# A GNN kernel's edge sort: four fifths moved from one-hot matmuls to indirect transfers into a DRAM table

## The reference, cut to what matters

```python
# GIN, twice:  agg[d] = sum over edges (s -> d) of h[s]
agg = jax.ops.segment_sum(h[src], dst, num_segments=n_nodes)
z = jax.nn.relu((agg + h) @ Wa + ba) @ Wb + bb
# attention, per edge, softmax over the edges of one head:
e = leaky_relu(sum((concat(x[head], x[tail]) @ W) * relation_emb[edge_type]))
alpha = softmax of e over each head;  agg[head] += alpha * x[tail]
```

## Time and profile before

| | |
|---|---|
| median of 3 runs | 5086.33 us (5085.47 to 5087.33) |
| profiled execution, span from first to last instruction | 4502.2 us |
| instructions | 61902 |
| mean granted TensorE clock | 0.671 of full speed |

### The profile page before, as it was taken

The page is one execution under the profiler, slowest core; times in us unless marked ns, Lnnn a source line. Parts: engine busy times, 40 slices in busy tenths (PEclk is TensorE's granted clock), DMA queues, the critical chain, the costliest instruction groups (busy, mean ns, idle before and its releaser), DMA issues. The chain is left out here.

```text
span 4502.2 us, 61902 instructions
## 1 busy us (share of the span) xinstructions
PE 3040.5 (68%) x16266; PEld 2267.0 (50%) x16267; DVE 3392.0 (75%) x7111; ACT 2104.7 (47%) x5569; POOL 1731.0 (38%) x1694
## 2 busy tenths in 40 slices
PE   5888888887255555555435555555546888779878
PEld 2444444466255555555435555555535888435434
DVE  8888888842588888888668888888858885444345
ACT  4555555551344444444345555555527885132231
POOL 0000000062577777777277777777700000021010
PEclk7999999988555555555555555555555555889988
DMA  0000000030322222222122222222230000000000
GB/s 21 0 0 0 0 0 0 0 161 1 69 67 67 67 67 67 67 67 69 31 71 66 69 67 67 67 67 67 63 162 1 1 1 2 11 4 1 4 9 8
DMA packets 136540, 183.42 MB, mean 41 GB/s; under 512 B 48763, under 2 KB 110116, under 8 KB 135396
## 3 DMA queue, kind: packets, MB, share of 16 engines
q0 software_dynamic: 50048, 77.77, 7.6%
q1 hardware_dynamic: 85348, 84.60, 6.9%
q10 hardware_dynamic: 896, 18.10, 0.9%
HBM read 158.02 MB, written 22.33 MB: 40 GB/s over the span
## 5 line engine op out<-in xcount | busy, mean ns | idle before, releaser
L1121 POOL DMA_INDIRECT adjacency<-dram_table,sorted_dst x1564 | 1555.9, 995 | 672.7 <-issue 425.8
L1148 PE MATMUL banks<-adjacency 128*128 x3520 | 779.5, 419 | 463.6 <-ACT adjacency L1180 463.6
L1148 PEld LDWEIGHTS banks<-adjacency 128*128 128x128 f32 x3520 | 759.3, 332 | 507.2 <-issue 507.2
L1193 ACT ACTIVATE adjacency<-adjacency 128x128 f32<-128x128 bf16 x1760 | 537.9, 397 | 50.2 <-DVE adjacency L1241 50.0
L1286 DVE TENSOR_REDUCE adjacency<-adjacency 128x512 f32<-128x2048 f32 x110 | 399.5, 3632 | 125.7 <-ACT adjacency L1193 125.7
L1180 ACT ACTIVATE adjacency<-adjacency 128x2048 f32<-128x2048 f32 x110 | 210.3, 1912 | 565.2 <-DVE adjacency L1218 565.2
L1921 PE MATMUL banks<-adjacency,cheb_parts 128*128 128x512 f16 (+1 forms) x2100 | 437.0, 367 | 52.5 <-ACTq L97 31.7
L665 ACT ACTIVATE adjacency<-banks 128x400 f32 x590 | 296.9, 503 | 318.6 <-PE banks L637 313.5
L1173 PE MATMUL banks<-ident,adjacency 128*128 128x128 f32 x440 | 122.6, 434 | 447.5 <-DVE adjacency L1286 447.5
L2190 POOL TENSOR_TENSOR cheb_y<-cheb_y,cheb_gain 128x512 f32<-128x512 f32 (+1 forms) x21 | 24.1, 1150 | 984.2 <-DVE cheb_y L2106 984.2
L634 PE MATMUL banks<-cell_hot,src_hot 128*128 128x400 f16 x1180 | 319.7, 353 | 74.0 <-DVE cell_hot L572 73.0
(11 more groups left out here) (497 smaller groups left out, 6100.8 us busy)
## 6 DMA issues: line engine op xcount, KB each, us to landing
adjacency<-dram_src_rows SPq DMA_DIRECT2D x440, 128.0 KB
adjacency<-dram_table,sorted_dst POOLq DMA_INDIRECT x1564, 2.5
dram_adjacency<-adjacency ACTq DMA_DIRECT2D x1, 17600.0 KB, 46.3
adjacency<-dram_adjacency SPq DMA_DIRECT2D x1, 15387.5 KB, 39.4
dram_table<-adjacency SPq DMA_DIRECT2D x8, 291.0 KB, 6.1
adjacency<-dram_adjacency SPq DMA_DIRECT2D x1, 2212.5 KB, 14.5
dram_nodes<-x_nodes SPq DMA_DIRECT2D x1, 800.0 KB, 4.3
x_nodes<-dram_nodes SPq DMA_DIRECT2D x1, 800.0 KB, 5.8
```

The lines of the kernel that those rows point to most:

```text
L1121: pool.indirect_dma_start(ring[:, j % (RG * TG), :], None, dram["table"], bass.IndirectOffsetOnAxis(ap=S.dst_i[:, j:j + 1], axis=0)).then_ ...
L1148: ins = pe.matmul(sums[b % 2][:, s * W1:(s + 1) * W1], reach[:, b % 3, s, t, :], ring[:, bass.ds(at_r[s], TG), :][:, t, 0:W1], start=(t == ...
L1193: ins = act.activation(reach[:, b % 3, s, t, :], hot[:, b % 2, s, :, t], ACT.Identity, scale=-FAR, bias=score[:, b % 2, s * TG + t:s * TG ...
```

## The change

**The sort** is split. `PG` = 157 groups (`PT` = 628 columns of edges) go another way; 39 groups (`LEFT_T` = 156 columns) stay with the one-hots. For the 628 columns GpSimd makes a payload of two fp16 numbers for each edge, VectorE makes the address in a DRAM table, `place_of` (lane times 782 plus tile), and GpSimd issues 628 indirect transfers of 128 elements of 4 bytes each into `dram_spread`, which SyncE has cleared with two transfers. At the group's start GpSimd waits for the group three earlier. At the end it waits for all and loads the table back into SBUF (`S.spread`). `sorted_edges` adds the loaded values to the one-hot part's.

**The loop** of `build_adjacency` now has turns of 15 steps with one group in each: 39 turns and a rest of 5 steps. Its registers are loaded for 5 steps at a time (`AT_ONCE`), so each turn has three `load_row` on VectorE, three on TensorE and nine on ScalarE. The pair buffers of the sort are single now, and the group's pieces stand at steps 0, 3, 6, 8, 9, 11 and 13 of the turn.

**The block bases** are made by VectorE inside the first convolution: four instructions at block 0 and one `scalar_tensor_tensor` of 782 columns at each block from 2 to 24, issued right behind `z` of that block.

GpSimd no longer takes part in the two meetings around `build_adjacency`.

```diff
+TURN, AT_ONCE = 15, 5
+ROUNDS = ASTEPS // TURN
+PG = NG - ROUNDS
+PT = PG * TG
+LEFT_T = TP - PT
 # rank_edges, on_sp
+        sp.wait_ge(k.V.sem, zeros_made[0])
+        for half in range(2):
+            sp.dma_start(clear[:, half * NT:(half + 1) * NT], zero[:, 0:NT // 2].bitcast(F16)).then_inc(zeros_out.sem, 16)
...
-    def lanes_dve(dve, half):
-    def tiles_dve(dve, half):
-    def rows_dve(dve, half):
+    def places_of(dve, half):
+        V = k.V
+        n = min(HALF, PT - half * HALF)
+        V(dve.tensor_copy(pos_i[:, 0, :], pos[:, half * HALF:(half + 1) * HALF]))
         V(dve.tensor_scalar(pos_i[:, 1, :], pos_i[:, 0, :], P - 1, None, ALU.bitwise_and))
         V(dve.tensor_scalar(pos_i[:, 0, :], pos_i[:, 0, :], 7, int(MARK) // P - 1, ALU.logical_shift_right, ALU.bitwise_and))
+        places_made.append(V.mark(dve.scalar_tensor_tensor(S.place_of[:, half * HALF:half * HALF + n], pos_i[:, 1, 0:n], float(NT),
+                                                           pos_i[:, 0, 0:n], ALU.mult, ALU.add)))
+    def rows_dve(dve):      # the same keys as before, for the last 156 columns alone, once
...
 # rank_edges, on_act, ahead of the second clearing
+        act.wait_ge(k.G.sem, payload_made[0])
+        act.wait_ge(zeros_out.sem, zeros_out.at(1))
 # rank_edges, on_pool
+        pool.wait_ge(cols_copied.sem, cols_copied.at(2 * RB - 1))
+        k.G(pool.tensor_scalar(S.payload[:, :, 0], dst_f[:, 0:PT], -float(NPAD // 2), None, ALU.add))
+        pool.wait_ge(k.V.sem, typed[0])
+        k.G(pool.tensor_scalar(S.payload[:, :, 1], src_b[:, 0:PT], -LO, None, ALU.add))
...
+        pool.wait_ge(k.V.sem, places_made[0])
+        for t in range(PT):
+            if t == HALF:
+                pool.wait_ge(k.V.sem, places_made[1])
+            g = t // TG
+            if t % TG == 0 and g >= LATE:
+                pool.wait_ge(scattered[(g - LATE) % TURNS].sem, scattered[(g - LATE) % TURNS].at(((g - LATE) // TURNS + 1) * TG - 1))
+            pool.indirect_dma_start(dram["spread"], bass.IndirectOffsetOnAxis(ap=S.place_of[:, t:t + 1], axis=0),
+                                    S.payload[:, t, :], None).then_inc(scattered[g % TURNS].sem, 16)
...
+        pool.dma_start(S.spread[:, :, :], dram["spread"].rearrange("(q c) v -> q c v", q=P)).then_inc(back.sem, 16)
 # build_adjacency
     def act_turn(act, turn, n):
-        first = turn * TURN
-        at_j = load_row(k, act, table[0:1, 1, bass.ds(first, n)], 0, NWIN - 1)
-        next_g = load_row(k, act, table[0:1, 0, bass.ds(first + AHEAD_R, n)], 0, TP - TGA)
-        next_j = load_row(k, act, table[0:1, 1, bass.ds(first + AHEAD_R, n)], 0, NWIN - 1)
+        for h in range(0, n, AT_ONCE):
+            now = turn * TURN + h
+            at_j = load_row(k, act, table[0:1, 1, bass.ds(now, AT_ONCE)], 0, NWIN - 1)
+            next_g = load_row(k, act, table[0:1, 0, bass.ds(now + AHEAD_R, AT_ONCE)], 0, TP - TGA)
+            next_j = load_row(k, act, table[0:1, 1, bass.ds(now + AHEAD_R, AT_ONCE)], 0, NWIN - 1)
+            for i in range(h, h + AT_ONCE):
...
 # block bases
-    for a in range(1, NB):
-        G(pool.tensor_scalar(beyond[:, :], place[:, :], S.block_start[:, a:a + 1], None, ALU.is_ge))
-        ins = pool.tensor_tensor(S.base[:, :], S.base[:, :], beyond[:, :], ALU.add)
+    def block(dve, a):
+        k.V(dve.scalar_tensor_tensor(S.base[:, :], place[:, :], S.block_start[:, a:a + 1], S.base[:, :], ALU.is_ge, ALU.add))
 # gin_conv, on_dve, stage 0
                 dve.tensor_tensor(z[:, i % R, :], psum[i % 2][:, 0:w], low[:, i % R, :], ALU.add).then_inc(z_made.sem, 1)
+                beside_dve(i)
 # sorted_edges
-    dve.tensor_copy(values[:, :, :], S.sorted[:, :, :])
-    dve.wait_ge(bases.sem, bases.at())
+    dve.wait_ge(back.sem, back.at())
+    dve.tensor_tensor(values[:, :, :], S.sorted[:, :, :], S.spread[:, :, :].rearrange("p t v -> p v t"), ALU.add)
```

More of the change, by code:

```diff
@@ L209, in rank_edges @@
     starts_made, starts_spread, cols_made = k.sig("starts_made"), k.sig("starts_spread"), k.sig("columns_made")
+    zeros_out, scattered, back = k.sig("spread_cleared", 16), [k.sig(f"tails{r}", 16) for r in range(TURNS)], k.sig("spread_in", 16)
+    zeros_made, typed, places_made, payload_made = [], [], [], []
     nodes_padded, nodes_in = k.sig("nodes_padded"), k.sig("nodes_in", 16)
@@ L360, in on_dve @@
                 dve.wait_ge(taken.sem, taken.at(i))
[L361 to L365, removed]
+                places_of(dve, 0)
             elif half == 1 and a == 14:
@@ L608, in pe_rows, with pe_tiles @@
+    def pe_rows(pe):
+        pe.wait_ge(group_valued.sem, 1)
         for t in range(TG):
-            ins = pe.matmul(part_v[0:ROWS, :], row_hot[:, 1 - g % 2, :, t], lane_value[:, 1 - g % 2, :, :, t], start=(t == 0), stop=(t == TG - 1))
+            ins = pe.matmul(part_v[0:ROWS, :], row_hot[:, :, t], lane_value[:, :, :, t], start=(t == 0), stop=(t == TG - 1))
         ins.then_inc(part_made.sem, 1)
-    def pe_tiles(pe, g, v, read, last=False):
-        b = 1 - g % 2
-        lanes = part[0:ROWS, b, v * P:(v + 1) * P]
+    def pe_tiles(pe, v):
+        lanes = part[0:ROWS, v * P:(v + 1) * P]
@@ L623, in pe_tiles @@
-        ins = pe.matmul(high_v[:, v * 256:(v + 1) * 256], lanes, tile_hot[0:ROWS, b, 512:768], start=False, stop=last and v == 1)
+        pe.matmul(low_v[v][:, :], lanes, tile_hot[0:ROWS, 0:512], start=False, stop=False)
+        ins = pe.matmul(high_v[:, v * 256:(v + 1) * 256], lanes, tile_hot[0:ROWS, 512:768], start=False, stop=False)
         if v == 1:
-            ins.then_inc(read.sem, 1)
+            ins.then_inc(tiles_read.sem, 1)
     def pe_turn(pe, turn, n):
-        first = turn * TURN
@@ L629, in pe_turn @@
-        at_j = load_row(k, pe, table[0:1, 1, bass.ds(first, n)], 0, NWIN - 1)
-        for i in range(n):
-            r = i % RING
-            pe.wait_ge(hot_made.sem, i + 1)
-            for t in range(TGA):
-                ins = pe.matmul(psum[r][:, 0:NB * WIN], one_b[:, r, :, t], one_c[:, r, t, :], start=(t == 0), stop=False)
-            ins.then_inc(hot_read.sem, 1)
-            pe.wait_ge(copied.sem, i + 1)
-            pe.matmul(psum[r][:, 0:NB * WIN], cst.ident16[:, :], A4[:, :, bass.ds(at_j[i], 1), :], start=False, stop=True).then_inc(done.sem, 1)
-            if n >= EACH:
-                g = i // EACH
-                if i % EACH == 0:
-                    pe_rows(pe, g)
-                else:
-                    pe_tiles(pe, g, i % EACH - 1, part_read)
+        for h in range(0, n, AT_ONCE):
+            at_j = load_row(k, pe, table[0:1, 1, bass.ds(turn * TURN + h, AT_ONCE)], 0, NWIN - 1)
+            for i in range(h, h + AT_ONCE):
+                r = i % RING
+                pe.wait_ge(hot_made.sem, i + 1)
+                for t in range(TGA):
+                    ins = pe.matmul(psum[r][:, 0:NB * WIN], one_b[:, r, :, t], one_c[:, r, t, :], start=(t == 0), stop=False)
+                ins.then_inc(hot_read.sem, 1)
+                pe.wait_ge(copied.sem, i + 1)
+                pe.matmul(psum[r][:, 0:NB * WIN], cst.ident16[:, :], A4[:, :, bass.ds(at_j[i - h], 1), :], start=False, stop=True).then_inc(done.sem, 1)
+                if n == TURN and i == ROWS_AT:
+                    pe_rows(pe)
+                elif n == TURN and i in SPREAD_AT:
+                    pe_tiles(pe, SPREAD_AT.index(i))
```

234 lines of the change are left out of this document (119 added, 115 removed).

## The result

The changed kernel took 6020.4 us in the median (6018.8 to 6020.7), the kernel before 5085.9 beside it: a ratio of 1.184 (1.182 to 1.185), 934 us slower. The prediction was 5192. The times come in two conditions.

What follows compares the result with a forecast made beforehand. Bound: the loop's chain of ScalarE copy, identity matmul and next copy. Loop +97, first convolution +13.5, small ones -5.1 give +105.4 on 5086.3: 5192 us, 8-in-10 range 5094 to 5265.

Steps and rivals of the forecast that it cites:

- I cost them at nothing: GpSimd's 628 transfers and their small writes, beside other work until the table is wanted at 1218 us: +0, at most +294.
- The runs' median lies 584.1 us above the span; I take that part as unchanged: Whole kernel: timed runs exceed the profiled span of 4502.2 us by 584.1, carried unchanged into the forecast time.
- That is 0.028 for a value, and 0.578 for 5: ScalarE's register loads in the loop: price per value, making three boundaries of a 15-step turn 7.73 us.
- The clock: Adjacency loop: mostly at half clock, a fifth of the time at 2.4 GHz, plain steps 1.28 us, mean near 0.6.
- Rival 1: Adjacency loop: the clock stays at 2.4 GHz, +11.4 us in all, a time of 5098; chance 0.13.
- VectorE off the path: Adjacency loop: VectorE does not set the pace; its pure step is some 0.67 us of the 1.28.
- The groups': Adjacency loop: 39 groups left of 196 on the one-hots, 157 x 0.31 = 49 us saved.
- The first convolution: VectorE's new instruction lengthens 23 blocks from 2.34 to 2.92 us: +13.5 us, bounds 0 and 23.
- The small ones: Rank stage, memsets, last group's tail and `sorted_edges`: small savings and costs summing to -5.1 us, bounds -8 and +3.
- the key operations: Rank stage, part of the small ones: fewer or narrower key operations on VectorE, said to save 4.1 us together.
- Rival 2: Attention layer waits for the table because GpSimd's transfers come late; at 2.3 us each +294, 5486 us; chance 0.10.
- Rival 3: Adjacency loop: register loads in the middle of a turn are hidden, loop -106 us, 4989 in all; chance 0.05.

Runs made afterwards that it cites:

- before_by_four: The kernel before with its register loads cut into fours, nothing else: 4482.3 against 4505.0 us (0.995) in the first condition, 5045.8 against 5067.3 (0.9955) in the second.
- twelve_by_four: The changed kernel with turns of 12 steps, loads of 4 values, 49 groups on TensorE: 4402.4 us against the kernel before's 4503.9; second condition 5675.6 against 5069.9.
- after_again: The changed kernel, unaltered, run again beside the kernel before, in the first condition: 4739.1 us against 4503.9, a ratio of 1.052.
- the execution of 5023.2 us: One of the four executions of `after_again`, the changed kernel unaltered; the other three took 4735.6 to 4741.6 us.
- before_again: The kernel before, unaltered, profiled once more: 4504.3 us with a span of 4502.7.

## Why the prediction was wrong, point by point

**"I cost them at nothing."** This is the step that failed in the measured times. Its own sum was right: 1.26 to 1.4 us for each, the last at about 920 us, wanted only at the end of the convolutions. What it left out is what the transfers do to the engines beside them: they hold up TensorE's hand-overs. I asked whether GpSimd would be late, and the place of the Trainium skill that I weighed ("SBUF — State Buffer", "Who interferes with whom") speaks of GpSimd kept waiting by VectorE. With the scatters beside the loop GpSimd was done by 923 us at the latest. The same section, which is about SBUF's ports, says that TensorE and ScalarE never wait on anyone; the hand-over of 6.5 us from one to the other beside the scatters is not in it. Price: 1755.4 - 1060.0 = 695 us of the 702; another 9 lie ahead of the first copy, which starts at 103.8 for 94.8 with the first scatters beside it.

**"The runs' median lies 584.1 us above the span; I take that part as unchanged."** Wrong as a reading. A span so far below its own kernel's times was the one sign in the profile that it was taken in another condition than the timed runs, and that something in the kernel was sensitive to it. From the first gather to the end the changed kernel loses 580 us by the condition and `before_by_four` 568, so the term nearly cancelled; had I asked what costs 584 us, the gathers were the candidate, and the change puts 628 of their kind beside the loop.

**"That is 0.028 for a value, and 0.578 for 5."** The line was drawn through loads of 2 and 12. What the runs show is 0.309 for 4 and 0.78 for 12 from a multiple of 4, 0.534 for 5 from such a place, 1.12 for 5 from another, 0.49 for 2. An estimate that fits all: from a first place that is a multiple of 4 the values come by fours, at some 0.24 to 0.31, and what is left singly at 0.22 to 0.25; from any other first place all come singly. The Trainium skill ("DMA: Bandwidth & Descriptors", "Latency and other measured facts") gives such a load a floor of about 600 ns; the trace doesn't agree (309 ns). The boundaries of four turns add up to 43.9 us, 10.97 a turn where I had 7.73: 39 x 3.24 = 126 us, and the loop was 1060.0 where I had 933. In the first condition this is the whole miss: 233 against 105.

**The clock** was right: plain steps at 1.28 us, those with spreading matmuls at 1.67, the one with the group at 1.89 for 1.85, a mean of 0.64 to 0.66. Rival 1 fell. It came back when the boundaries shrank, at 0.98 in `twelve_by_four`. **VectorE off the path** was right: in `after_again` it is busy for 522.6 of the loop's 1060 us. **The groups'** saving of 49 us is in no row by itself.

**The first convolution** was right in mechanism and nearly in size: the new instruction starts every 2.95 us (I had 2.92), +10.4 to +12.5 us where I had +13.5. **The small ones** gave -2.3 at the first copy and nothing after it that can be told apart, for -5.1; the forecast's own parts of the key operations, 1.0, 2.4 and 0.5, add up to 3.9 and not 4.1. From the last copy to the first gather it is 224.0 us in `before_again` and 234.9 in `after_again`. With +224.0 for the loop: 224.0 + 10.9 - 2.3 = 232.6, the difference of the two spans, 4735.3 - 4502.7.

**Rival 2** named GpSimd and the right side, by a mechanism that did not occur. **Rival 3** fell for loads of 5; with loads of 4 a boundary inside a turn takes 1.42 us for a plain step's 1.11, nearly hidden.

Still open: what puts an execution in the one condition or the other (one chip showed both, and the execution of 5023.2 us fits neither), whether the late hand-over is a late end of a matmul or a late signal, and why the first plain transfers were like indirect ones. No run here tells these apart.

## What to carry to other kernels

Ask of a hidden transfer not only whether it is done in time but what it does to the engines beside it: put a few of its kind beside the loop in a throwaway kernel, in several sessions, before moving 628. A profile whose span differs from the timed runs by more than some microseconds may be of another condition, and the gap is to be located, not carried along. Load registers in fours from places that are multiples of four, and keep the batches small enough to lie behind other work.

## What the runs showed of the hardware

While GpSimd's indirect transfers ran beside the changed kernel's loop, the semaphore that TensorE counts up for ScalarE came 6.9 to 18.9 us after the start of its matmul in one of two conditions, and after 0.35 to 0.56 in the other; one chip showed both conditions. In the one run that had them in the condition of the hold-up, transfers from SyncE's queue and GpSimd's arithmetic did not do it. A register load of five values took 0.53 us or 1.12, by where it starts, and one of four 0.31.
